# Message stage of a graph network: where sums, squares and one-hots are kept and how they are formed

## The reference, cut to what matters

```python
def _mlp(h, W, b, gamma, beta):
    h = jax.nn.relu(h @ W + b)
    mu = jnp.mean(h, axis=0)
    var = jnp.mean(jnp.square(h - mu), axis=0)
    return gamma * (h - mu) * jax.lax.rsqrt(var + EPS) + beta

node_feat = _mlp(x, W_node, b_node, g_node, beta_node)
edge_feat = _mlp(edge_attr, W_edge, b_edge, g_edge, beta_edge)
message = jnp.concatenate([x[row], x[col], edge_feat], axis=1)
message = _mlp(message, W_msg, b_msg, g_msg, beta_msg)
agg = jax.ops.segment_sum(message, col, num_segments=n)
return agg + node_feat
```

## Time and profile before

| | us |
|---|---|
| three runs, median | 2734.09 |
| three runs, lowest and highest | 2731.89, 2740.01 |
| the profiled execution | 2738.54 |
| its span, first to last instruction | 2736.8 |
| PE busy in it | 1948.0 (71%) |
| DVE busy | 1399.4 (51%) |
| POOL busy | 1033.7 (38%) |
| ACT busy | 788.3 (29%) |
| all gathers of the message stage, busy | 858.6 |

### The profile page before, as it was taken

The page is one execution under the profiler, slowest core; times in us unless marked ns, Lnnn a source line. Parts: engine busy times, 40 slices in busy tenths (PEclk is TensorE's granted clock), DMA queues, the critical chain, the costliest instruction groups (busy, mean ns, idle before and its releaser), DMA issues. The chain is left out here.

```text
span 2736.8 us, 50828 instructions
## 1 busy us (share of the span) xinstructions
PE 1948.0 (71%) x15395; PEld 1609.1 (59%) x15396; DVE 1399.4 (51%) x2745; ACT 788.3 (29%) x1385; POOL 1033.7 (38%) x1171
## 2 busy tenths in 40 slices
PE   1777777776999999968855665566666666655488
PEld 0333344445999999964534555555555555555477
DVE  7866866666444434456554444444444444444653
ACT  1587466662111111112122222222222222222320
POOL 3211221114000000000007777777777777777300
PEclk9987988886999999988975766666666666666699
DMA  3311111111000000080013222222222222221200
GB/s 125 107 50 46 39 49 58 58 57 44 2 2 2 2 2 2 15 305 1 3 38 55 55 53 54 53 52 53 52 53 52 52 53 54 53 53 48 74 1 19
...
## 3 DMA queue, kind: packets, MB, share of 16 engines
...
...
## 5 line engine op out<-in xcount | busy, mean ns | idle before, releaser
L1376 POOL DMA_INDIRECT counts<-p_rows,rows x784 | 858.6, 1095 | 239.4 <-issue 238.5
L1590 PE MATMUL ps_e_seg<-counts 128*128 128x96 f32 x1568 | 355.9, 420 | 408.8 <-ACT counts L1529 408.8
L1590 PEld LDWEIGHTS ps_e_seg<-counts 128*128 128x128 f32 x1568 | 335.3, 325 | 453.1 <-issue 453.1
L928 PE MATMUL ps_hop<-y,counts 128*128 128x192 f16 x6250 | 527.5, 248 | 25.7 <-DVEq L815 13.8
L928 PEld LDWEIGHTS ps_hop<-y,counts 128*128 128x128 f16 x6250 | 522.0, 99 | 31.0 <-DVEq L815 13.9
L1422 DVE TENSOR_TENSOR counts<-ps_e_z,counts 128x768 f32<-128x768 f32 x98 | 93.9, 958 | 589.0 <-DMA counts<-p_rows,rows 584.6
L558 DVE TENSOR_TENSOR hot_w<-iota_w,places_now 128x1600 f16<-128x1600 f16 x300 | 297.0, 990 | 186.0 <-PE ps_counts L584 175.0
L584 PE MATMUL ps_counts<-hot_w,hot_p 128*128 x1196 | 300.0, 385 | 125.0 <-DVE hot_p L558 80.7
L1529 ACT ACTIVATE counts<-counts 128x768 f32<-128x768 f32 x98 | 82.6, 843 | 810.1 <-DVE counts L1422 807.8
L1379 POOL MEMSET e_attr<- 39x3072 bf16 x1 | 2.7, 2651 | 761.7 <-POOLq L1103 761.7
L525 POOL TENSOR_TENSOR places_now<-places,origins (+1 forms) x302 | 110.9, 368 | 463.1 <-DVE hot_p L558 274.6
...
## 6 DMA issues: line engine op xcount, KB each, us to landing
...
counts<-p_rows,rows POOLq DMA_INDIRECT x784, 2.5
...
```

Of the source, the lines that this page charges most:

```text
L928: mm = pe.matmul(ps[:, r, 0:2 * D], k.counts[:, m, b, :], y[:, odd, b, :], start=b == 0, stop=b == NB - 1)
L1376: nc.gpsimd.indirect_dma_start(z[:, slot, j, :], None, k.p_rows, bass.IndirectOffsetOnAxis(rows, 0)) \
L1590: mm = pe.matmul(ps_s[:, two, 0:D], hot[:, two, j, :], z[:, slot, j, :], start=j == 0, stop=j == STEP_TILES - 1)
```

## The change

What it does, by place:

- The gathered rows are added onto `ps_z` in PSUM, not onto the slot in SBUF. POOL then waits for that addition (`z_added`) alone before it fills the slot again.
- The message after the ReLU is kept as two fp16 numbers, a high half by ACT and the remainder by DVE (`low_half`), side by side in `split`; one fp16 matmul of 192 columns with an fp16 one-hot takes the place of the fp32 one of 96, into one bank, and DVE joins the two halves of the result (`joined`) into `step_sum` before it goes to totals and blocks.
- ACT applies the ReLU a second time, in fp32, for the squares. Their sum lies in a bank of PSUM (`ps_sq`), half as wide, and is added to in two instructions.
- Each one-hot is made by several comparisons with one scalar a partition (8 for the places, 4 for the nodes), from `place_of` and `span_of`, fp32 copies made at the stage's start.
- So that fp16 can hold them, the messages are scaled: POOL and PE bound their size from the weights in `prepare_messages`, DVE forms `unit` and its inverse and scales weights and bias; `gcn_layers` takes the unit out again.
- The fill of `attr` with ones has gone from POOL to DVE.

```diff
@@ prepare_messages
+        @block.gpsimd
+        def _(pool):
+            size = Chain(pool, sized)
+            size(nc.gpsimd.memset(ln_reach, LN_MOST))
+            pool.wait_ge(w_in, 16 * 7)
+            size(nc.gpsimd.tensor_scalar(w_size, w[0:D, 0:2 * D], 0.0, -2.0, ALU.min, ALU.mult))
+            size(nc.gpsimd.tensor_tensor(w_size, w_size, w[0:D, 0:2 * D], ALU.add))
...
+            size(nc.gpsimd.tensor_copy(all_reach, edge_reach.broadcast_to([D, P])))
@@ DVE, behind the layer norm
+            dve.wait_ge(limited, 1)
+            step(nc.vector.tensor_scalar(k.unit[:, :], ps_bn[:, 0, 0:D], 1.0 / HALF_MOST, 1e-30, ALU.mult, ALU.max))
+            step(nc.vector.reciprocal(scale[:, :], k.unit[:, :]))
+            nc.vector.tensor_tensor(w[0:D, 0:2 * D].rearrange("p (a f) -> p a f", a=2),
+                                    w[0:D, 0:2 * D].rearrange("p (a f) -> p a f", a=2),
+                                    scale[0:D, :].unsqueeze(1).broadcast_to([D, 2, D]), ALU.mult).then_inc(scaled, 1)
+            nc.vector.tensor_tensor(k.w_part[:, :], k.w_part[:, :], scale[0:D, :], ALU.mult)
             dve.wait_ge(shift_done, 1)
-            nc.vector.tensor_tensor(bias_row[:, 1, :], bias_row[:, 0, :], ps_c[:, 0:D], ALU.add).then_inc(const_ready, 1)
+            step(nc.vector.tensor_tensor(bias_row[:, 1, :], bias_row[:, 0, :], ps_c[:, 0:D], ALU.add))
+            nc.vector.tensor_tensor(bias_row[:, 1, :], bias_row[:, 1, :], scale[0:1, :], ALU.mult).then_inc(const_ready, 1)
@@ pass_messages, POOL
-            nc.gpsimd.memset(attr[:, :, :], 1.0).then_inc(pool_made, 1)
...
-                    pool.wait_ge(squared, s - SLOTS + 1)
-                    pool.wait_ge(seg_done, s - SLOTS + 1)
+                    pool.wait_ge(z_added, s - SLOTS + 1)
@@ DVE
-                nc.vector.tensor_tensor(u_hot[D:P, two, :].rearrange("p (n e) -> p n e", n=Q_SPANS),
-                                        dst_rows[D:P, fed, :].rearrange("p (n e) -> p n e", n=Q_SPANS),
-                                        nodes, ALU.is_equal).then_inc(turned, 1)
+                for n in range(Q_SPANS):
+                    mine = slice(n * Q_TILES * P, (n + 1) * Q_TILES * P)
+                    made = nc.vector.tensor_scalar(u_hot[D:P, two, mine], dst_rows[D:P, fed, mine], nodes(n), None,
+                                                   ALU.is_equal)
+                made.then_inc(turned, 1)
...
-                nc.vector.tensor_tensor(hot[:, two, :, :], k.iota_p[:, :].unsqueeze(1).broadcast_to([P, STEP_TILES, P]),
-                                        places.unsqueeze(2).broadcast_to([P, STEP_TILES, P]), ALU.is_equal) \
-                    .then_inc(hot_ready, 1)
+                for j in range(STEP_TILES):
+                    made = nc.vector.tensor_scalar(hot[:, two, j, :], k.iota_p[:, :], places(j), None, ALU.is_equal)
+                made.then_inc(hot_ready, 1)
...
-                nc.vector.tensor_tensor(halves(z[:, slot, :, :]), ps_z[:, two, :, 0:HALF_BANK], halves(z[:, slot, :, :]),
-                                        ALU.add).then_inc(z_added, 1)
+                nc.vector.tensor_tensor(ps_z[:, two, :, 0:HALF_BANK], ps_z[:, two, :, 0:HALF_BANK],
+                                        halves(z[:, slot, :, :]), ALU.add).then_inc(z_added, 1)
...
-                nc.vector.tensor_tensor(sq_sum[:, :, :], sq_sum[:, :, :], z_sq[:, :, :], ALU.add).then_inc(sq_added, 1)
+                nc.vector.tensor_tensor(sq_sum, sq_sum, halves(z_sq)[:, 0, :], ALU.add).then_inc(sq_half, 1)
+                dve.wait_ge(sq_half, s + 1)
+                nc.vector.tensor_tensor(sq_sum, sq_sum, halves(z_sq)[:, 1, :], ALU.add).then_inc(sq_added, 1)
+
+            def low_part(two):
+                return nc.vector.scalar_tensor_tensor(by_half(split[:, two, :, D:2 * D]), by_tile(two), 0.0,
+                                                      by_half(split[:, two, :, 0:D]), ALU.max, ALU.subtract)
...
-                nc.vector.tensor_tensor(k.totals[:, 0, :], ps_s[:, s % 2, 0:D], k.totals[:, 0, :], ALU.add)
+                nc.vector.tensor_reduce(step_sum[:, :], joined(), AX.X, ALU.add).then_inc(seg_joined, 1)
+                dve.wait_ge(seg_joined, s + 1)
+                nc.vector.tensor_tensor(k.totals[:, 0, :], step_sum[:, :], k.totals[:, 0, :], ALU.add)
                 for n in range(2):
-                    added = nc.vector.scalar_tensor_tensor(sums[n], ps_s[:, s % 2, 0:D], k.part_masks[:, n, s:s + 1],
+                    added = nc.vector.scalar_tensor_tensor(sums[n], step_sum[:, :], k.part_masks[:, n, s:s + 1],
                                                            sums[n], ALU.mult, ALU.add)
...
+            nc.vector.memset(attr[:, :, :], 1.0).then_inc(ones_set, 1)
...
+            nc.vector.tensor_copy(span_of[:, :, :], k.span_node[:, :, :])
+            nc.vector.tensor_copy(place_of[:, :], k.place_h[:, :])
@@ ACT
-            def rectified(s, slot):
+            def rectified(s, two):
                 act.wait_ge(z_added, s + 1)
-                nc.scalar.activation(z[:, slot, :, :], z[:, slot, :, :], ACT.Relu).then_inc(z_relu, 1)
+                if s >= 2:
+                    act.wait_ge(seg_done, s - 1)
+                nc.scalar.activation(by_half(split[:, two, :, 0:D]), by_tile(two), ACT.Relu)
+                act.wait_ge(sq_added, s + 1)
+                nc.scalar.activation(halves(z_sq), ps_z[:, two, :, 0:HALF_BANK], ACT.Relu).then_inc(z_relu, 1)
                 act.wait_ge(z_relu, s + 1)
-                act.wait_ge(sq_added, s + 1)
-                nc.scalar.activation(z_sq[:, :, :], z[:, slot, :, :], ACT.Square).then_inc(squared, 1)
+                nc.scalar.activation(z_sq[:, :, :], z_sq[:, :, :], ACT.Square).then_inc(squared, 1)
@@ PE
                 if s >= 2:
-                    pe.wait_ge(z_added, s - 1)
+                    pe.wait_ge(z_low, s - 1)
...
-                pe.wait_ge(z_relu, s + 1)
+                if s:
+                    pe.wait_ge(seg_joined, s)
+                pe.wait_ge(z_low, s + 1)
                 for j in range(STEP_TILES):
-                    mm = pe.matmul(ps_s[:, two, 0:D], hot[:, two, j, :], z[:, slot, j, :], start=j == 0,
+                    mm = pe.matmul(ps_s[:, 0:2 * D], hot[:, two, j, :], split[:, two, j, :], start=j == 0,
@@ gcn_layers, DVE
+            step(nc.vector.tensor_tensor(norm[:, 2, :], k.unit[:, :], k.unit[:, :], ALU.mult))
+            dve.wait_ge(msg_in, 32)
+            step(nc.vector.tensor_tensor(msg_rows[:, 0, :], msg_rows[:, 0, :], k.unit[:, :], ALU.mult))
             dve.wait_ge(totaled, 1)
...
-            nc.vector.tensor_scalar(norm[:, 1, :], norm[:, 1, :], 0.0, BN_EPS, ALU.max, ALU.add).then_inc(asked, 1)
+            step(nc.vector.scalar_tensor_tensor(norm[:, 1, :], norm[:, 1, :], 0.0, norm[:, 2, :], ALU.max, ALU.mult))
+            nc.vector.tensor_scalar(norm[:, 1, :], norm[:, 1, :], BN_EPS, None, ALU.add).then_inc(asked, 1)
...
-            dve.wait_ge(msg_in, 32)
```

101 lines of the change are left out of this document (71 added, 30 removed).

## The result

The changed kernel takes **2620.0 us** (median of 4 runs, 2613.2 to 2627.7), the kernel before, run beside it, 2737.1 us (4 runs, 2731.9 to 2741.3). The ratio is 0.9577, with a 95% interval of 0.9550 to 0.9603: 4.2% faster, 117 us. The forecast was 2668 and its range ended at 2628. The direction was right; the gain was nearly twice what the sum gave (117 us for 66), and the time lies outside the range.

What follows compares the result with a forecast made beforehand. The prediction took POOL's queue of gathers in the message stage as the bound. Its terms, -118 + 49 - 0.8 + 0 - 0.5 + 2.0 + 2.6, gave -66 us: 2668 us against the median, range 2628 to 2712.

Steps and rivals of the forecast that it cites:

- What bounds the kernel: Message stage: a queue of 784 + 8 gathers on POOL, each its duration plus 0.30 us; the surplus is 118 us.
- What makes the surplus: Message stage: about 0.13 us after its start a gather waits out a DVE instruction with two SBUF inputs; removal -118 us.
- The +49 us for the short instructions: Message stage: new sums and one-hot comparisons delay gathers by 0.50 us a step, 49 us; the sums alone 10 us.
- the prediction's own formula: Message stage: with gather moments 1.25 us apart, a DVE instruction of length d costs d x d / 2.5 on average.
- The comparisons don't contend at all: Message stage: comparisons hold no gather, only the sums' 10 us stay; 2629 us, range 2622 to 2650, chance 0.17.
- A gather holds what it has taken: Message stage: a gather blocks comparisons for its remaining 0.81 us; cost 83 us, time 2702, chance 0.25.
- Change of owner: Message stage: twelve short holds cost as much as three long ones, or DVE and POOL end level; 2712 to 2742, chance 0.10.
- DVE becomes the bound: Message stage: comparisons wait for gathers until DVE's step exceeds POOL's; +141 us, 2875, chance 0.10.
- Preparation: Between the layer norm's end and the bias row's DMA: five small DVE instructions add 2.0 us.
- End of the stage: After the last rows of the message stage: more DVE work, shorter matmuls, one reduction for three adds; about -0.5 us.
- Start of the stage: Message stage start: POOL's fill goes, but DVE's fill, copy and casts delay the ninth gather's row list; 0, bounds -3 and +3.
- The norm of the last layers: Last layers: the wait for the message rows' DMA moves ahead, with a product and one more instruction; +2.6 us.

Runs made afterwards that it cites:

- old_release: The changed kernel, with POOL waiting again for the squares and segment sums before it refills a slot: 2621.4 us, ratio 0.9570.
- place_long: The changed kernel, with the eight place comparisons of a step put back as one two-input comparison of 1024 elements: 2695.9 us, ratio 0.9839.
- node_long: The changed kernel, with the four node comparisons of a step put back as one two-input comparison of 1024 elements: 2656.4 us, ratio 0.9706.
- slow_read: The changed kernel plus, at each step's end, a one-input DVE sum along the row of 1056 elements, in the slow form: 2624.9 us, ratio 0.9584.
- long_copy: The changed kernel plus, at each step's end, a DVE copy of 2112 fp32 elements onto themselves: 2700.8 us, ratio 0.9876.
- node_split: The changed kernel, with the node one-hots made by four two-input comparisons of 256 elements: 2635.3 us, ratio 0.9633.
- scalars_alone: The kernel before, with only its two one-hots made by comparisons with a scalar (8 of 128, 4 of 256): 2643.6 us, ratio 0.9663.
- better_d: The changed kernel, with the last messages' wait moved to just before their use and the attr ones written as half as many 32-bit elements: 2616.6 us, ratio 0.9563.

## Why the prediction was wrong, step by step

**What bounds the kernel: right.** A queue of gathers on POOL with a surplus of 118 us; L1429's rows after show 949 ns for 1095, the fixed pause unchanged, and DVE still waiting for rows. old_release shows that the slots had no part in it.

**What makes the surplus: right, and not sharp enough.** Two-input instructions with both inputs in SBUF hold a gather at 0.13 us after its start. place_long, node_long and slow_read bear it out: put one back and the surplus is back, with an instruction as long but of one input and in the slow form it isn't. But the hold begins only 0.126 us after the instruction's recorded start, and which instruction holds how much is set by its place. I had read the place in the earlier trace rows, where the gather of 2006.64 starts 0.22 us into L1407, and didn't ask why it does so in each step. It does: 0.96 us behind L1407 in the mean of 98 steps of before, and only 0.23 behind L1415. 94 of the 118 us stood behind one instruction.

The Trainium skill (SBUF — State Buffer, "Who interferes with whom") infers that `tensor_tensor` doesn't stall descriptor generation. At a gather's first point the runs contradict it (0.66 us a step in place_long); at the second point they agree (96 of 97 gathers in before, during which L1415 started, took 0.94 to 0.95 us), and they bear out that the fast copy does stall it there. That whoever starts first shuts the other out for the whole instruction is not so here for a gather: the copy of long_copy took its 1.26 us though it started 0.37 us into one, and only what comes in a gather's last part is held.

**The +49 us for the short instructions: the step that failed.** It should have been 2.5 at most, the surplus of all gathers of after behind the first one, of which 0.96 is L1543's. Two things were wrong in it, and both made it too large. First, its length: I took the whole recorded duration d. A held gather shows what counts, the stretch at the end of the instruction in which a point is held. Gathered over all traces of the study:

```
instruction of VectorE                 recorded     points held    points free
two inputs in SBUF, 1024 elements      1.22 us      last 1.09      all earlier
two inputs in SBUF, 256 elements       0.42 us      last 0.26      0.33 and more before its end
one input and a scalar, 256, fast      0.35 us      last 0.12      0.19 and more before its end
one input and a scalar, 128, fast      0.25 us      last 0.07      0.09 and more before its end
  (one gather of node_split, held for 0.12, is left out; with fp32 out 0.28 us, last 0.13)
masked add, 96 elements                0.31 us      last 0.12      0.16 and more before its end
```

In the rest of a short instruction's record nothing is held. With these lengths in the prediction's own formula the sum is (3 x 0.12^2 + 8 x 0.07^2 + 4 x 0.12^2) / 2.5 = 0.06 us a step, 5.5 us for 98, where the recorded durations gave 49. In a square, a duration that is three times too long costs nine times too much.

Second, the chance. The three adds of the sums, to which I gave 10 us as the least, stand in after at 2210.42 to 2211.13, between the points 2210.21 and 2211.46 of two gathers, and so in nearly every step: they cost nearly nothing (0.15 us by L1506 in 98 steps, none by L1508). Together the gathers behind the first show 2.5 us of surplus.

I had seen that the same formula gave 1.56 us a step for the three old instructions where 1.2 is measured, and called that a sign of no underestimate. It was the sign of an overestimate, and of a formula for chance on something that wasn't.

**The rivals.** "The comparisons don't contend at all" came nearest, with 0.17 for its chance and 2622 as its lower end; even that is above the 2620 measured, because it kept the 10 us of the sums. "A gather holds what it has taken" fell with long_copy for the 0.81 us that it named; for the last part of a gather it is so. "Change of owner" is there in scalars_alone, for 27 us, and is gone in after, where the squares lie in PSUM. "DVE becomes the bound" did not come near: a step of DVE takes 131/200 of 10 us, 6.5 where 7.7 was forecast, and it waits 296 us for rows. What it named, comparisons waiting for gathers, does occur. The medians hide it, their longest don't (ns, shortest, median, longest):

```profile
L1469 DVE TENSOR_SCALAR counts<-iota_p,e_place_of x784: 237/248/500, 1480.7 to 2431.9; 128x128 f16<-128x128 f16 x196
L1460 DVE TENSOR_SCALAR counts<-e_dst_rows,e_span_of x392: 340/347/574, 1479.3 to 2425.1; 32x256 f32<-32x256 f16 x196
```

But the delays come to 0.17 us a step in all, where this rival needed more than 3.5.

**The rest of the sum: within 0.5 us a term, but for the start of the stage.** Preparation +2.0, measured 1386.16 - 1384.10 for the bias row's DMA, 2.06 (columns: start, duration):

```profile
1384.39 0.75 DVE L1212 RECIPROCAL seg<-unit 128x96 f32<-128x96 f32 x1
1385.17 0.35 DVE L1213 TENSOR_TENSOR w<-w,seg 96x192 f32<-96x192 f32 x1
...
1386.16 0.61 SPq L1160 DMA_DIRECT2D w<-bias_row  x1
...
1388.04 0.63 PE L1283 MATMUL ps_t<-ident_f,h 128*96 128x128 f32 x2 [6.86 <-DMA w<-bias_row]
```

It answers to the earlier trace rows, two us later. End of the stage -0.5, measured -0.8. Start of the stage 0, bounds -3 and +3: measured -0.4 to the first gather and +2.7 for its 4.24 us in the place of 1.49, so +2.3. That lies within the bounds, but for a reason that the prediction didn't have: not the ninth gather waited, for its row list, but the first one, held beside the fill. The norm of the last layers +2.6, measured +3.1, by the wait that was named, to the earlier trace rows:

```profile
2447.67 0.42 SPq L1766 DMA_DIRECT2D msg_rows<-in_L_gnn_beta_msg  x1
...
2450.67 0.26 DVE L1860 TENSOR_TENSOR msg_rows<-msg_rows,unit 128x96 f32<-128x96 f32 x1 [2.79 <-DMA msg_rows<-in_L_gnn_beta_msg]
```

better_d moves that wait and has 2.4 us of it back. With what was measured in the place of each term, in the prediction's order, the sum is -118 + 2.5 - 0.5 (the pauses, with the one wait for a slot) + 2.3 - 0.8 + 2.0 + 3.1 = -109, and the profiled executions differ by 110.9.
